# Flamingo cross-attention and FFN block on one core: rank weights on 128 partitions with one DMA per group, and three warm-up calls in place of five

## What is computed

```python
xn    = layernorm(x)                                    # eps 1e-5
q_hk  = (xn @ Wq.T).reshape(b, s, 16, 128)              # 16 heads
q_big = einsum('bshk,hkq->bshq', q_hk, w_kc_q)          # rank 192
q_r   = einsum('bshq,hqr->bhsr', q_big, W_qr)           # 64
k_r   = einsum('bld,hdr->bhlr', rope(ctx), W_kr)
attn  = softmax(einsum('bhsr,bhlr->bhsl', q_r, k_r))
ctx_c = einsum('bhsl,bld->bhsd', attn, rope(ctx))
x    += tanh(g_xattn) * (einsum('bhsd,hkd->bshk', ctx_c, w_kc_kv).reshape(b, s, 2048) @ Wo.T)
y     = layernorm(x); t = in_norm(y)[:, -1] @ agg_w + agg_b
for _ in range(4):
    t += gelu(layernorm(t) @ d1_w + d1_b) @ d2_w + d2_b
x    += tanh(g_ffn) * out_norm(y + sigmoid(y @ gate_w + gate_b) * (t @ bc_w + bc_b))
```

## Time and profile before

| | us |
|---|---|
| runs shown (3) | median 212.63, 212.58 to 213.01 |
| the profiled execution | 213.38 |
| its span, first to last instruction | 211.4 |
| PE busy in the span | 193.6 (92%) |
| DVE busy | 169.2 (80%) |
| ACT, POOL busy | 96.6 (46%), 71.9 (34%) |
| mean granted TensorE clock | 0.949 of full |
| DMA queue q1 | 17.46 MB, 28.5% of 16 engines |

### The profile page before, as it was taken

How to read it: one execution, slowest core, us unless ns; L and a number is a source line. 1 busy time by engine, 2 the same in 40 slices (tenths; PEclk the granted TensorE clock), 3 DMA queues, 4 the chain that set the end, 5 groups by cost and what they waited for, 6 DMA issues and landing times.

```text
span 211.4 us, 6214 instructions
## 1 busy us (share of the span) xinstructions
PE 193.6 (92%) x2533; PEld 169.7 (80%) x2533; DVE 169.2 (80%) x399; ACT 96.6 (46%) x177; POOL 71.9 (34%) x151
## 2 busy tenths in 40 slices
PE   7289979999999999999999999999999999998860
PEld 5078969679889997889999998999887888887730
DVE  4742699999799999996995999395973787899975
ACT  2215354443954355555193567548325243471120
POOL 5520147999006899600203200020000130702443
PEclk9855899999999999999999999999998799999995
DMA  6999996404065004100120120000071001010001
GB/s 172 229 250 337 416 416 238 102 5 99 3 199 105 0 5 102 51 3 3 33 72 3 28 75 5 3 0 3 5 172 31 2 3 51 0 44 13 25 25 50
DMA packets 10499, 17.85 MB, mean 84 GB/s; under 512 B 1052, under 2 KB 6436, under 8 KB 9960
## 3 DMA queue, kind: packets, MB, share of 16 engines
q1 hardware_dynamic: 10472, 17.46, 28.5%
HBM read 12.15 MB, written 1.05 MB: 62 GB/s over the span
## 4 chain that ended last, share of the span: by engine, by line
PE 57%; DVE 20%; POOL 8%; DMA 5%; issue 5%; ACT 2%; SPq 1%; POOLq 0%; DVEq 0%; ACTq 0%
PE ps L1032 9%; PE ps L1019 7%; PE ps L1000 6%; PE ps L1021 6%; PE ps L900 4%; DMA wqr<-in_wqr 4%; PE ps L901 4%; PE ps L902 4%; PE ps L936 4%; DVE row_max L749 3%; DVE bn L675 2%; PE ps L1121 2%; PE ps L1110 2%; PE ps L1081 2%; PE ps L1042 2%
## 5 line engine op out<-in xcount | busy, mean ns | idle before, releaser
L638 ACT ACTIVATE probs<-ps 128x512 f32<-128x512 f32 x64 | 36.2, 596 | 33.8 <-PE ps L1021 32.9
L749 DVE TENSOR_REDUCE row_max<-ps 128x2 f32<-128x512 f32 x64 | 41.7, 681 | 5.6 <-PE ps L1000 5.1
L556 POOL TENSOR_SCALAR var_eps<-mean_var 128x1 f32<-128x1 f32 (+1 forms) x29 | 7.3, 251 | 114.0 <-DVE mean_var L676 113.4
L1032 PEld LDWEIGHTS ps<-kv,probs 128*64 128x64 f32 x1024 | 31.2, 137 | 3.0 <-issue 2.0
L1032 PE MATMUL ps<-kv,probs 128*64 128x65 f32 x1024 | 33.6, 223 | 0.0
L1019 PE MATMUL ps<-q_hi,kv_lo 128*128 128x512 f32 x64 | 28.3, 443 | 0.2 <-DMA q_hi<-shift 0.2
L1021 PE MATMUL ps<-q_split,kv_hi 128*128 128x512 f32 x64 | 25.5, 398 | 0.0
L1000 PE MATMUL ps<-kv_hi,q_split 128*128 128x256 f32 x128 | 24.9, 300 | 0.4 <-DVE q_split L743 0.4
L1000 PEld LDWEIGHTS ps<-kv_hi,q_split 128*128 128x128 f32 x128 | 19.1, 189 | 3.9 <-issue 1.9
L900 PE MATMUL ps<-xT_lo,A_hi 128*128 128x256 f32 x64 | 18.9, 295 | 0.1
L900 PE MATMUL ps<-B_lo,ctxT_hi 128*128 128x256 f32 x64 | 18.5, 289 | 0.0
(11 more groups left out here) (133 smaller groups left out, 405.7 us busy)
## 6 DMA issues: line engine op xcount, KB each, us to landing
q_hi<-q_split SPq DMA_DIRECT2D x16, 256.0 KB, 4.1
wq<-in_wq SPq DMA_DIRECT2D x4, 512.0 KB, 12.5
woT<-in_woT SPq DMA_DIRECT2D x2, 1024.0 KB, 18.0
w_rest<-in_d_w SPq DMA_DIRECT2D x2, 1024.0 KB, 12.8
wkcqT<-in_wkcqT SPq DMA_DIRECT2D x4, 384.0 KB, 8.8
out_x<-fin SPq DMA_DIRECT2D x8, 128.0 KB
wqr<-in_wqr SPq DMA_DIRECT2D x4, 192.0 KB, 10.1
x<-in_x SPq DMA_DIRECT2D x2, 256.0 KB, 10.3
```

Source lines behind the costliest of these rows:

```text
L638: act.activation(probs[:, n % PROBS_BUFS, lb, :], bank(e), ACT.Exp).then_inc(free[place[e]], 1)
L749: dve.reduce_max(row_max[:, s % 2, 2 * j:2 * j + 2], bank(e).rearrange("p (h l) -> p h l", h=2), AX.X).then_inc(free[place[e]], 1)
L1032: ins = pe.matmul(bank(e)[q:q + 64, hh * (DC + 1):(hh + 1) * (DC + 1)], probs[:, n % PROBS_BUFS, lb, hh * P + q:hh * P + q + 64], kv1[:, k ...
```

## The change

- The weights of `qrT` come in one array `rank`, laid out on the host for pairs of heads on 128 partitions, and are fetched by one DMA per group (640 KB: 128 partitions with 5120 contiguous bytes each) in place of `wqr` (192 KB) and `wkcqT` (384 KB). The rank of 192 is now split as 128 and 64; the part of 64 of an even head lies on partitions 0 to 63 and that of the odd head on 64 to 127, with zeros on the other half of the `queries` operand's partitions, so that both can be multiplied with one shared `keys` operand.
- `wkrT` (256 KB, 64 partitions) becomes `wkr` (512 KB, 128 partitions), block diagonal for a pair of heads, half of it zeros. `qk` then makes 4 matmul calls of 128 partitions by 128 columns in place of 8 of 64 by 64. `qrT` makes 8 calls as before, with 128 in place of 96 partitions.
- ACT copies all of `qrT`'s result in one instruction; the four DVE copies and their semaphore are gone.
- WARM is 3 in place of 5.
- Most slots of SLOTS are new.

```diff
-JQ = DCQ // 2
+RANK = 3 * P + 4 * R
-WARM = 5
+WARM = 3
...
-        wkrT = sb("wkrT", [R, H * DC], F32, stage)
-        wqr = sb("wqr", [JQ, H, 2, R], F32, stage)
-        wkcqT = sb("wkcqT", [JQ, H, 2, P], F32, stage)
-        qrT = sb("qrT", [R, 2, HG * P], F32, stage)
+        wkr = sb("wkr", [P, H // 2, 2 * DC], F32, stage)
+        rank = sb("rank", [P, H // 2, RANK], F32, stage)
+        qrT = sb("qrT", [P, 2, HG // 2 * P], F32, stage)
...
+                if name == "load_wkr":
+                    sp.dma_start(wkr[:, :, :], t["wkr"]).then_inc(wkr_in, 16)
+                if name == "load_rank":
+                    ps2 = slice(HG // 2 * e[1], HG // 2 * (e[1] + 1))
+                    sp.dma_start(rank[:, ps2, :], t["rank"][:, ps2, :]).then_inc(rank_in[e[1]], 16)
...
                 if name == "qrT":
                     filled(act, e)
-                    act.activation(qrT_cols(e[1], 1), bank(e)[upper, 0:HG // 2 * P].rearrange("p (i k) -> p i k", k=P),
-                                   ACT.Copy).then_inc(qrT_odd_copied, 1)
+                    act.activation(qrT[:, e[1] % 2, :], bank(e)[:, 0:HG // 2 * P], ACT.Copy
+                                   ).then_inc(free[place[e]], 1)
...
-                if name == "qrT":
-                    dve.wait_ge(qrT_odd_copied, e[1] + 1)
-                    filled(dve, e)
-                    dve.tensor_copy(qrT_cols(e[1], 0), bank(e)[lower, 0:HG // 2 * P].rearrange("p (i k) -> p i k", k=P)
-                                    ).then_inc(free[place[e]], 1)
...
                     g = e[1]
-                    pe.wait_ge(wqr_in[g], 16)
-                    pe.wait_ge(wkcqT_in[g], 16)
-                    for hh in range(0, HG, 2):
-                        for j in range(2):
+                    pe.wait_ge(rank_in[g], 16)
+                    for i in range(HG // 2):
+                        w = rank[:, HG // 2 * g + i, :]
+                        for part in range(2):
                             for odd in range(2):
-                                ins = pe.matmul(bank(e)[64 * odd:64 * odd + 64, hh // 2 * P:(hh // 2 + 1) * P],
-                                                wqr[:, HG * g + hh + odd, j, :], wkcqT[:, HG * g + hh + odd, j, :],
-                                                start=(j == 0), stop=(j == 1))
+                                keys = w[:, P:2 * P] if part else w[:, 2 * P * odd:2 * P * odd + P]
+                                queries = w[:, 3 * P + R * (2 * part + odd):3 * P + R * (2 * part + odd + 1)]
+                                ins = pe.matmul(bank(e)[64 * odd:64 * odd + 64, i * P:(i + 1) * P], queries, keys,
+                                                start=(part == 0), stop=(part == 1))
...
-                    for hh in range(HG):
-                        h = HG * g + hh
+                    for i in range(HG // 2):
                         for k in (0, 64):
-                            ins = pe.matmul(bank(e)[k:k + 64, hh * DC:(hh + 1) * DC],
-                                            qrT[:, g % 2, hh * P + k:hh * P + k + 64],
-                                            wkrT[:, h * DC:(h + 1) * DC], start=True, stop=True)
+                            ins = pe.matmul(bank(e)[k:k + 64, 2 * i * DC:2 * (i + 1) * DC],
+                                            qrT[:, g % 2, i * P + k:i * P + k + 64],
+                                            wkr[:, HG // 2 * g + i, :], start=True, stop=True)
```

More of the change, by code:

```diff
@@ L47 @@
 KEEP = 5
-WARM = 5
+WARM = 3
 SLOTS = {
     "pe": {
-        "kvT": (0, 3),
-        "qrT": (1, 2, 7, 8),
+        "kvT": (1, 3),
+        "qrT": (0, 2, 7, 13),
         "qk": (4, 5, 10, 14),
[L55 to L62, removed]
[5 rows of a table removed]
[L68 to L80, removed]
@@ new lines @@
+        "foldA": (8, 9, 15, 16),
+        "foldB": (23, 25, 32, 35),
+        "xT": (6, 24, 44, 139),
+        "gq": (11, 12, 19, 22, 28, 31, 37, 41, 86, 89, 96, 97, 160, 161, 170, 195),
+        "smax": (17, 18, 20, 21, 26, 27, 29, 30, 33, 36, 38, 42, 43, 47, 48, 52, 54, 57, 59, 62, 63, 67, 70, 71, 75,
+            77, 80, 82, 83, 85, 87, 88, 94, 95, 98, 99, 107, 112, 114, 120, 121, 124, 126, 130, 136, 148, 152, 153, 165,
+            166, 171, 173, 179, 187, 202, 204, 208, 214, 215, 219, 222, 224, 226, 229),
@@ L81 @@
+        "down": (135, 156, 186, 203),
+        "downT": (138, 159, 189, 212),
+        "bc": (220,),
+        "bc_rows": (225, 227, 228),
+        "keep": (277,),
     },
     "dve": {
[L83 to L90, removed]
@@ L102 @@
-        "c_norm": (87, 99, 119, 140, 163),
-        "thoughtT": (91, 102, 121, 142, 165, 181),
+        "kvT": (2, 5),
+        "foldA": (7, 9, 19, 22),
+        "foldB": (28, 31, 39, 45),
+        "x_stats": (0, 1, 8, 10, 11, 12, 13, 18),
+        "x_norm": (3, 4, 16, 17, 36, 37, 57, 60),
+        "xT": (6, 27, 48, 121),
+        "gq": (14, 15, 25, 26, 34, 35, 42, 49, 77, 80, 87, 88, 140, 141, 147, 168),
+        "smax": (20, 21, 23, 24, 29, 30, 32, 33, 38, 40, 41, 43, 44, 46, 47, 50, 51, 54, 55, 59, 61, 62, 64, 65, 67,
[4 rows of a table added]
@@ L112 @@
+        "f_norm": (196, 201, 206, 213, 218, 226, 242, 243),
     },
     "act": {
[L114 to L122, removed]
[3 rows of a table removed]
-        "ctxT": (40, 43, 61, 62, 70, 72, 89, 93, 108, 110, 123, 125, 135, 143, 144, 145),
@@ L127 @@
-        "yT": (63, 79, 103, 119, 132, 136, 146, 147),
-        "gate": (82, 105, 130, 131, 137, 142, 148, 149),
-        "up": (66, 73, 91, 101),
-        "bc_rows": (115, 116, 118),
+        "g_tanh": (11,),
+        "kvT": (1, 3),
+        "qrT": (0, 2, 7, 14),
+        "qk": (4, 5, 10, 15),
+        "foldA": (8, 9, 16, 17),
+        "foldB": (21, 22, 26, 27),
+        "xT": (6, 20, 31, 74),
+        "gq": (12, 13, 18, 19, 23, 24, 28, 34, 51, 52, 55, 56, 85, 86, 90, 103),
+        "shiftT": (25, 37, 48, 59, 67, 88, 109, 125),
[3 rows of a table added]
@@ L1174, in columns @@
         return np.concatenate([a["L0_ffn_" + n].reshape(-1, P) for n in names], axis=0).T
+    keys = a["L0_xattn_w_kc_q"].transpose(0, 2, 1)
+    queries = a["L0_xattn_W_qr"]
+    rank = np.zeros((H // 2, P, RANK), np.float32)
+    wkr = np.zeros((P, H // 2, 2 * DC), np.float32)
+    for odd in range(2):
+        rows = slice(64 * odd, 64 * odd + 64)
+        wkr[rows, :, DC * odd:DC * (odd + 1)] = a["L0_xattn_W_kr"][odd::2].transpose(2, 0, 1)
+        rank[:, :, 2 * P * odd:2 * P * odd + P] = keys[odd::2, 0:P]
+        rank[:, rows, P:2 * P] = keys[odd::2, P:DCQ]
+        rank[:, :, 3 * P + R * odd:3 * P + R * (odd + 1)] = queries[odd::2, 0:P]
+        rank[:, rows, 3 * P + R * (2 + odd):3 * P + R * (3 + odd)] = queries[odd::2, P:DCQ]
     late = a["x"][:, P:, :].reshape(NB, 2, 2, QB, D).transpose(0, 3, 1, 2, 4)[:, :, ::-1].reshape(P, NB, D)
@@ L1179, in laid_out @@
         "ctx": a["ctx_512"].reshape(NB, LB, P, DC).transpose(2, 0, 1, 3),
-        "wkrT": a["L0_xattn_W_kr"].transpose(2, 0, 1).reshape(R, H * DC),
-        "wqr": a["L0_xattn_W_qr"].reshape(H, JQ, 2, R).transpose(1, 0, 2, 3),
-        "wkcqT": a["L0_xattn_w_kc_q"].reshape(H, K, JQ, 2).transpose(2, 0, 3, 1),
+        "wkr": wkr,
+        "rank": rank.transpose(1, 0, 2),
         "wq": a["L0_xattn_Wq"].reshape(H, K, D).transpose(1, 0, 2),
```

121 lines of the change are left out of this document (61 added, 60 removed), and 24 rows, old and new, of the table SLOTS.

## The result

The changed kernel takes **206.17 us** (median of 4 runs, 205.52 to 207.67) where the kernel before, on the same chip, takes 212.61 us (4 runs, 212.18 to 213.01): a ratio of 0.971 [0.965, 0.977], 6.4 us less. A later session of 6 and 19 runs gives 206.07 and 212.49, again 6.4 us. The kernel before scatters by itself, between 207.5 and 216.2 us in the three later sessions, with the clock that it is granted.

A forecast was written before the change was run, and what follows sets the result against it. A late start bounds, then DVE to 45 us and PE to 190, so a lead carries through. From the median, 212.63 - 5.5 (earlier first `foldA`) + 0.0 for other edits and POOL = 207.1 us, range 203.2 to 210.8.

The forecast's parts named there:

- The loads.: Start: narrow transfers run at 239 GB/s, 128-partition ones at 409; `rank0` lands at 5.5 us in place of 11.2.
- rival (3): Start: the slow rate belongs to the first 18 us, not the partitions; lead 4.1, 208.5 us; chance 0.04.
- I take 409 GB/s: Load queue from 3.9 us on: every load moves at 400 KB per us, which gives all forecast landing times.
- PE up to the first foldA.: PE's list to `foldA0` takes 12.6 us at half clock, ending at 18.1 in place of 23.67: 5.5 us earlier.
- rival (1): Start: full clock in part or all of it; lead up to 9.3, 203.3 to 206 us; chance 0.27.
- The lead at the first `A_lo` is what I carry to the end.: From 24.3 us to the end: DVE, then PE, bound without room, so the 5.5 us lead stays whole.
- POOL.: Before `y_norm0`: POOL's root comes 54.4 us behind `A_lo`; DVE's stand is 0 to 2.5 us, taken as 0.
- Rival (2): Middle: lead shrinks, `y_stats0` costs 2.5 us in full, `smax` steps another microsecond; 209.5 to 211; chance 0.16.
- The other edits.: Warm calls, DVE copies, `g_tanh`, `out` and moved loads: off the path or hidden, `g_tanh` costing 0.2 us; total 0.0.
- (4): Past `foldA`, into `gq` and `smax`: clock stays at 1.2 GHz; low until 40 us gives 217; chance 0.04.
- (5): Middle 145 us: the new slot order is by itself worse than the lead is long; 213 to 215; chance 0.04.

The follow-up runs named there:

- in halves: The changed kernel with each `rank` and `wkr` transfer issued as two of 64 partitions, one after the other: 212.45 us.
- `x0` first: The changed kernel with the load of `x0` issued ahead of `rank0`: 207.72 us.
- form alone: The new arrays, transfers, matmul calls and ACT copy in the slot order of the kernel before, five warm-up calls: 208.39 us against 212.64.
- order-alone: The kernel before, its transfers, calls and copies put in the new slots, five warm-up calls: 214.10 us against 212.64.
- filled one: The kernel before with eight more matmul calls on zeros between `kvT0` and the first `qrT`: 209.54 us against 211.44.
- stats late: The changed kernel with the statistics of units 4 to 7 moved behind the first folds and `smax` steps on DVE and POOL: 209.70 us.

## Why the prediction was right, and where it was not

The forecast of 207.1 us stands 0.9 above the median of 206.17, inside its range. The mechanism behind it is only partly what happened: two of its steps were wrong by some three microseconds each, in opposite directions, and that they nearly cancel is luck.

**"The loads."** The form of the transfer is what costs, and 128 partitions move at the full rate: 401 GB/s from 9 to 21 us with 409 forecast, 292 with the same bytes in halves. That also settles rival (3), the slow rate as a property of the first 18 us, for all but the first 9. But the list was wrong from its first line: `rank0` at 8.1 in place of 5.5, `x0` 11.2 in place of 7.7, `wkr` 12.4 (9.0), `wq0` 15.3 (11.9), the rows 19.5 (16.1), `rank3` 21.4 (17.7), `wo1` 32.5 (29.2), some 3.4 us late from `x0` on. The failing step is "I take 409 GB/s" from 3.9 us on. In the first 9 us the engines move 224 GB/s, 2.0 MB, where my rule has 2.5; that is some 1.3 us. The rest, about 2 us by the same sum, lies between the time at which the rates say that the bytes have moved and the landing that the waiting engine sees, and I had no term for it. Both are estimates from the rows' rates. The trace shows what the second is made of. Each load raises its semaphore in sixteen steps, and the engine waits for the last. Those of `rank0` come from 5.72 us on, the fifteenth at 7.16, the sixteenth at 8.13; those of `x0` from 8.83, the fifteenth at 10.26, the sixteenth at 11.20. So a load is spread over some 2.4 us, while the rate already counts the bytes of the next one. In the second execution of the same kernel `rank0` is spread from 5.34 to 8.06, without the gap before the last. The trace of before had the warning: its `wkcqT0` landed at 7.7, where even 239 GB/s from 3.9 us on give 5.5. I had checked the rule against the rate of a later stretch and never against a landing. The Trainium skill ("SBUF — State Buffer", the section on the DMA setup-cost knee) adds about 2 us to the bytes over 436 GB/s. By it, taken as an estimate for the 1088 KB up to `rank0` as one transfer issued at 0.7 us, they would be in at about 5.3, no later than by my rule; the trace disagrees with both.

**"PE up to the first foldA."** I took the list of 12.6 us at half clock throughout. Half clock held for 3.4 us only (7.7 to 11.1), and from `qrT0`'s start to `foldA0`'s end it was 8.95 us, 3.7 less. This is the condition of rival (1), which had 0.27, together with its mechanism: at full clock DVE holds the list up, through `x0`'s statistics and norm to `xT0` at 14.49. Only that DVE waited for `x0` and not for its own memset. The argument that tipped me, that the clock before stayed low for 11 us of work and so would again, fell. In the kernel with `x0` first it was low up to 14.5, in form alone from 12.2 to 19.0, with nine warm calls not at all after 5.8; what the clock does at the start does not follow from the steps alone.

The two errors: `A_lo` at 18.7 was forecast, 17.76 came; lead 5.5 forecast, 6.6 measured, 7.6 at the end of the profiled execution and 6.4 in the medians. With the loads as late as they were and the clock as low as I had it, `A_lo` would have come at 8.2 + 12.6 + 0.6 = 21.4, a lead of 2.9.

**"The lead at the first `A_lo` is what I carry to the end."** It agreed here and isn't true in general. In the order-alone kernel a lead of 3.9 at `A_lo` is none at `row_max`, in the filled one 4.3 becomes 2.0. What carries is `row_max`, 7.0 earlier here, and then `y_norm0` through POOL.

**"POOL."** The right place and nearly the right numbers. `w_parts` start 9.6 us after `A_lo` (10.1 forecast) and the root ends 52.7 after it (54.4), the second load taking 4.9 beyond POOL's last part of the first half. The stall of 0 to 2.5 us, taken as 0, was 0.15. But to call it hidden was too kind: there is no slack at all, and 3.7 us on that chain were 3.6 on the kernel. Rival (2) was near, and "stats late" is what it looks like.

**"The other edits."** Taken at nothing, and rightly: three, five and nine warm calls are the same; `g_tanh` came at 19.54, just before `gq0`'s copy at 20.25; POOL's `out` ran at 19.95 to 21.8, with `x_stats3` after it. Of `qk` and `qrT` no call takes longer on 128 partitions: a `qrT` at half clock is 1.97 to 1.98 in both forms and 1.09 at full clock.

**Rivals (4) and (5)**, a clock low until 31 us and an order bad by itself: the clock was full from 11.1. The second is half true: the new order with the old transfers is 1.5 us slower than before. With the new ones it gains about 2.

So of the 6.4 us in the medians, 4.25 are the form with the old order and 1.8 to 2.3 the new order on top of it. The clock's part is inside these. In the profiled executions the low stretch at the start is 13.7 us long before, 6.8 in form alone and 3.4 in the changed kernel; but it is 10.2 in order alone, whose first `qrT` begins at 7.6 too, so the earlier `qrT` alone doesn't keep the clock, and what does isn't shown. By itself, in the old kernel, the clock is worth 1.9.

The kernel before, in its quickest executions, runs at 207.5 to 208.2, and the quickest runs of the changed one are at 205.5. Against the quickest executions of the session form alone has a ratio of 0.993 [0.986, 1.001], the changed kernel with five warm calls 0.988 [0.978, 0.998], and the changed kernel itself 0.990 [0.985, 0.994]. I read it so that some 2.5 us of the gain are there in every execution, and the rest is what the kernel before mostly pays for a low clock at its start and the changed one doesn't; how long the clock was low in the runs without a profile isn't recorded, only its mean.

## What to carry to other kernels

Check a forecast of a load's landing against a landing in the trace, not only against a rate: a rate of 400 GB/s later on said nothing about the first 9 us, and a load that has moved on the mean still waits for its last sixteenth. Carry a lead from the last point at which every late input has arrived (here the first `row_max`), and follow the helper engine's chain beside it, since an engine that is busy a third of the time can still have no slack where it matters. A reordering that pulls the first step forward pays only if the loads of the steps that it pushes back still come in time.
